# An attention and expert kernel on one core: the attention loop written out, four pieces of a step in another place

## The chip, the core and the metric

The kernel runs on one core of a Trainium2 chip. The time is the device time of one execution in microseconds, and the median of several executions is what counts. Before the change it is 2137.03 us, the median of three runs (2134.46 to 2138.43). TensorE (PE) multiplies, VectorE (DVE), ScalarE (ACT) and GpSimd (POOL) do the rest, and SyncE (SP) issues most of the transfers.

## The reference

Input `x` has 32 batches of 128 rows and 512 columns. The first half is attention with 32 heads of 16 columns, with a second set of keys and values from the adapter `ctx`; the second half is a mixture of 8 experts, of which each row uses two.

```python
q, k, v = (split_heads(layernorm(x) @ W) for W in (Wq, Wk, Wv))
q, k = rope(q), rope(k)
w = softmax(q @ k.T * D ** -0.5 + mask)
a_k, a_v = split_heads(ctx @ Wk), split_heads(ctx @ Wv)
a = tanh(gate) * softmax(q @ a_k.T * D ** -0.5)
x = x + merge_heads(w @ v + a @ a_v) @ Wo
h = layernorm(x)
top2, ids = top_k(h @ router_w.T, 2)
out = x + sum(softmax(top2)[j] * expert(ids[j], h) for j in (0, 1))
# expert(e, h) = (silu(gate_e(h)) * up_e(h)) @ w2[e].T
```

## The kernel before

`program` runs `attention_phase` and then `expert_phase`; the change is in the first alone. A batch is one tile of 128 rows. In float16 a product is made of three (high by high, high by low, low by high), so a projection of 512 columns is 12 matmuls (`project`, L1045), and a tensor that goes into one is first split: ACT writes the high half, POOL or DVE the difference.

Each engine has its own program. `walk` (L244) calls an engine's `step(b, c, d, n, m)` once for each batch b, with its neighbours: c is two batches back, d one back, n the next and m the one behind that. A step finishes batch b (softmax and values), projects the output of d and normalizes it (h), enters the rows of c in the lists of the experts, and prepares n (projections of queries, keys, adapter keys, stacks of heads, the maxima of the scores). Nothing but the order of the calls in `step` and the semaphores sets the order of the work: every engine takes its instructions in the order in which they stand. Steps 4 to 27 are a hardware loop of three rounds with eight steps each (`eng.Fori`, `LOOP`), all other steps are written out.

TensorE's step has 16 rounds u, one for each half group of heads: `scores_T` (L1143, L1147, L1152) writes scores in `st`, ACT takes their exponentials (`exps`, L561), and `values` for round u-1 (L1166) multiplies them by the values. Other pieces lie between: in round 2 `k` (projection of the keys of n, in `ma[1]`) ahead of values 1 and `out_turn` (the output's transposes, L1039, in `md[0]`) behind it; in round 3 `out_project`; in round 4 `ak` (adapter keys); `stack` (L1084) from round 6 on; `h_turn` in round 7 and `router` in round 8.

ACT's step is not touched by the diff. In round 2 it has, in this order, the third exponential (L561), `w_slice` (two passes over a slice of the experts' weights, L571 and L572) and `out_T` (L583), which copies the output's transposes to `oT` for `out_project`. Later come `k_high` (L539), `ak_high` (L519) in round 4, `h_high` (L589) in round 5, the first `values_T` (L567), the exponential of round 6, the first `stack_out` (L553, L555), the exponential of round 7, and `h_transposed` (L594), for which `router` waits. The exponential of round u waits for `scores_T` of round u.

VectorE's step has `router_top` (L838 to L861, the choice of two experts for c), `rotate_k` (L730, L734), `router_weights`, `residual` (L809 to L817), `router_counts` (L866, L868), `router_rows` (L906 to L915, places in the lists), `norm_h` (L824), `ak_low` (two L721, which `stack` 0 on TensorE waits for), `h_low` (L829), `norm_x` (L693), `normal` 0 (L786 to L798), `router_logits` (L833), and then the maxima (L754, L756, L759) of the eight groups. The adapter scores of group 0 (L1108) use the bank that `router_logits` reads, and wait for it.

GpSimd's step has `q_sum` (L410), `q_low` (L415), `w_slice` (L448), `k_sum` (L420), `norm_h`, `k_low` (L425), `x_low` (L405) and `enter_lists`.

Of the kernel before, what the change touches and what calls it, by code (L numbers as in the profile page):

```python
# [24 lines left out]
NB = 32  # L25
# [12 lines left out]
GROUPS = NH // 4  # L38
VW = HD + 1
VC = 32  # L40
LOOP = 8
LB = 4
SLOTS = 2 * T // P + NE - 1
TAB = 16
# [59 lines left out]
def attention_phase(nc, ctx, dram, keep):  # L104
# [139 lines left out]
    def whole(n):  # L244

        return isinstance(n.n, int) and n.n == 0

    def walk(eng, step, first, last):

        def near(b, lacks):
            step(b, *(None if d in lacks else b.shift(d) for d in (-2, -1, 1, 2)))

        first(Batch(0, 0))
        near(Batch(0, 0), (-2, -1))
        near(Batch(0, 1), (-2,))
        near(Batch(0, 2), ())  # L260
        near(Batch(0, 3), ())
        with eng.Fori(0, (NB - 8) // LOOP) as it:
            for k in range(LOOP):
                near(Batch(it, 4 + k, LOOP), ())
        near(Batch(0, NB - 4), ())
        near(Batch(0, NB - 3), ())
        near(Batch(0, NB - 2), (2,))
        near(Batch(0, NB - 1), (1, 2))
        last(Batch(0, NB - 1))

    def heads(t):
        return t[:, :].rearrange("p (h d) -> p h d", d=HD)
# [392 lines left out]
    def _(dve):  # L665
# [116 lines left out]
        def normal(n, o):  # L782

            bank = av[o % 2][:, :, :].rearrange("p (a g) (j c) -> p a (g j) c", a=2, c=VC)
            dve.wait_ge(v_back.sem, v_back.at(n, o + 1))
            dve.reciprocal(rc[:, :, :], bank[:, :, :, HD]).then_inc(n_rc.sem, 1)  # L786
            dve.wait_ge(n_rc.sem, n_rc.at(n, o + 1))
            dve.tensor_tensor(rc[:, 1, :], rc[:, 1, :], tg[:, 8 * o:8 * o + 8], ALU.mult).then_inc(n_rg.sem, 1)
            dve.wait_ge(n_rg.sem, n_rg.at(n, o + 1))
            dve.tensor_tensor(part2[:, :, :, :], bank[:, :, :, 0:HD],  # L790
                              rc[:, :, :].unsqueeze(3).to_broadcast([P, 2, 8, HD]), ALU.mult).then_inc(n_o2.sem, 1)
            dve.wait_ge(n_o2.sem, n_o2.at(n, o + 1))
            if o == 0:
                if whole(n):
                    dve.wait_ge(list_pad.sem(n), list_pad.at(n))
                dve.wait_ge(o_hi.sem, o_hi.at(n.shift(-1)))
                dve.wait_ge(o_lo.sem, o_lo.at(n.shift(-1)))
            dve.tensor_tensor(heads(on)[:, 8 * o:8 * o + 8, :], part2[:, 0, :, :], part2[:, 1, :, :],  # L798
                              ALU.add).then_inc(n_o.sem, 1)

        def out_low(n):
            dve.wait_ge(o_hi.sem, o_hi.at(n))
            dve.tensor_tensor(ohs[:, 1, :], on[:, :], ohs[:, 0, :], ALU.subtract).then_inc(o_lo.sem, 1)
# [15 lines left out]
        def norm_h(n, x_batch):  # L819
            dve.wait_ge(h_rs.sem, h_rs.at(n))  # L820
            if x_batch:
                dve.wait_ge(x_hi.sem, x_hi.at(x_batch))
                dve.wait_ge(x_lo.sem, x_lo.at(x_batch))
            dve.tensor_scalar(nat[:, :], x2[:, :], mv[:, 1, 0:1], mv[:, 1, 3:4], ALU.subtract,  # L824
                              ALU.mult).then_inc(h_n.sem, 1)

        def h_low(n):
            dve.wait_ge(h_hi.sem, h_hi.at(n))
            dve.tensor_tensor(ohs[:, 1, :], nat[:, :], ohs[:, 0, :], ALU.subtract).then_inc(h_lo.sem, 1)  # L829
# [64 lines left out]
        def router_rows(n):  # L894

            if whole(n):
                dve.tensor_scalar(unsel[:, :], sel[:, :], -1.0, 1.0, ALU.mult, ALU.add).then_inc(f_step.sem, 1)
                dve.wait_ge(f_step.sem, f_step.at(n, 1))
                dve.scalar_tensor_tensor(out=pos[:, :], in0=unsel[:, :], scalar=tok[:, 1:2], in1=pos[:, :],
                                         op0=ALU.mult, op1=ALU.add).then_inc(f_step.sem, 1)  # L900
                dve.wait_ge(f_step.sem, f_step.at(n, 2))
                dve.tensor_tensor(pos[:, :], pos[:, :], ebase[:, :], ALU.add).then_inc(f_step.sem, 1)
                dve.wait_ge(f_step.sem, f_step.at(n, 3))
                dve.tensor_copy(posi[:, :], pos[:, :]).then_inc(f_pos.sem, 1)
            else:
                dve.tensor_tensor(pos[:, :], pos[:, :], ebase[:, :], ALU.add).then_inc(f_step.sem, 1)  # L906
                dve.wait_ge(f_step.sem, f_step.at(n, 1))
                dve.tensor_tensor(chosen[:, :, :], oh[:, :, :], pos[:, :].unsqueeze(1).to_broadcast([P, 2, NE]),
                                  ALU.mult).then_inc(f_step.sem, 1)
                dve.wait_ge(f_step.sem, f_step.at(n, 2))  # L910
                dve.tensor_reduce(place[:, :], chosen[:, :, :], AX.X, ALU.add).then_inc(f_step.sem, 1)
                dve.wait_ge(f_step.sem, f_step.at(n, 3))
                dve.tensor_copy(posi[:, 0:2], place[:, :]).then_inc(f_pos.sem, 1)

            dve.tensor_scalar(tok[:, 0:1], tok[:, 0:1], float(P), None, ALU.add).then_inc(f_step.sem, 1)  # L915
            dve.wait_ge(f_step.sem, f_step.at(n, 4))

        def step(b, c, d, n, m):
            if n:
                ctx_lo(n)  # L920
                mask_lo(n)
                rotate_q(n)
            if d:
                out_low(d)
            if m:
                stats_x(m)
            if c:
                router_top(c)
            if n:
                rotate_k(n)  # L930
            if c:
                router_weights(c)
            if d:
                residual(d)
            if c:
                router_counts(c)
                router_rows(c)
            if d:
                norm_h(d, n)
            if n:  # L940
                ak_low(n)
            if d:
                h_low(d)
            if m:
                norm_x(m)
            normal(b, 0)
            if d:
                router_logits(d)
            if n:
                maxima(n, 0)  # L950
                maxima(n, 1)
            normal(b, 1)
            if n:
                for g in range(2, 6):
                    maxima(n, g)
            normal(b, 2)
            if n:
                for g in range(6, GROUPS):
                    maxima(n, g)
                neg_max(n, b)  # L960
            else:
                normal(b, 3)
# [72 lines left out]
    def _(pe):  # L1035
# [25 lines left out]
        def k(n):  # L1061
            pe.wait_ge(av_v.sem, av_v.at(n.shift(-1)))
            project(ma[1], xT, wk).then_inc(k_p.sem, 1)
# [113 lines left out]
        def out_turn(n):  # L1177
            pe.wait_ge(o_hi.sem, o_hi.at(n))
            pe.wait_ge(o_lo.sem, o_lo.at(n))
            transposes(md[0], ohs).then_inc(o_tp.sem, 1)  # L1180
# [24 lines left out]
        def step(b, c, d, n, m):  # L1205
            if n:
                q(n)
            for u in range(2 * GROUPS):
                scores_T(b, u)
                if u in BACK_AT:  # L1210
                    values_back(b, BACK_AT.index(u))
                if u == 2 and n:
                    k(n)
                if u == 3 and d:
                    out_project(d)
                if u == 4 and n:
                    ak(n)
                if u == 7 and d:
                    h_turn(d)
                if u == 8 and d:  # L1220
                    router(d)
                if n and u in STACK_AT:
                    stack(n, STACK_AT.index(u))
                if n and u in SCORES_AT:
                    adapter_scores(n, SCORES_AT.index(u))
                if u:
                    values(b, u - 1)
                if u == 2 and d:
                    out_turn(d)
                if u == 3 and c:  # L1230
                    places(c, n)
                if n and u in SCORES_AT:
                    own_scores(n, SCORES_AT.index(u))
            if n:
                v(n)
                adapter_scores(n, GROUPS - 1)
            values(b, 2 * GROUPS - 1)
            if n:
                own_scores(n, GROUPS - 1)
            if m:  # L1240
                x_turn(m)
            if n:
                avp(n)
            values_back(b, 3)
            if n:
                max_turn(n)
# [385 lines left out]
```

## Time and profile before

| | |
|---|---|
| median of three runs | 2137.03 us (2134.46 to 2138.43) |
| profiled execution | 2133.7 us, of which the span of the instructions is 2131.9 us |
| PE busy | 1900.5 us, 89% |
| DVE busy | 1452.3 us, 68% |
| ACT busy | 1219.3 us, 57% |
| POOL busy | 647.5 us, 30% |
| mean granted clock of TensorE | 0.975 |

The attention phase takes the first 1645 us or so and the experts the rest. In the written rows a time is a place on the span's clock. Busy shares are means over both phases; which engine ends a wait is read in the list of waits and in the timeline. Matmuls overlap, so the start of the next one lies a little ahead of the modelled end of the one in front.

### The profile page before, as it was taken

The page shows a single profiled execution, that of the slowest core. Times are in us where ns is not written, and L with a number is a line of the kernel's source. Part 1 is how long each engine was busy: PE and PEld are TensorE (multiplying, and loading weights), DVE is VectorE, ACT ScalarE, POOL GpSimd, SP SyncE. Part 2 cuts the span into 40 slices and gives each one's busy share as a digit, 9 for nine tenths or more (in the row PEclk, how much of TensorE's full clock was granted, in tenths as well). Part 3 has the DMA queues.
Part 4 walks back from the last instruction along what each step waited for, and adds up shares of the span by engine and source line. Part 5 has one row for each costly group of instructions (what it writes and reads, how often), then busy time and mean ns, then how long its engine had stood idle before and what let it go on. Part 6 is the DMA issues. An engine that isn't in the chain of part 4 may idle for free. (4 is left out here: it accounts for less than half of the span.)

```text
span 2131.9 us, 54083 instructions
## 1 busy us (share of the span) xinstructions
PE 1900.5 (89%) x18697; PEld 1172.2 (55%) x18698; DVE 1452.3 (68%) x3621; ACT 1219.3 (57%) x2228; POOL 647.5 (30%) x667
## 2 busy tenths in 40 slices
PE   4898899989998999999899999999983799999997
PEld 2555555555554555555555555555551466666664
DVE  5577788888887888888788888888874333333332
ACT  4565566666665666666566666666662434434342
POOL 3123233222322222232222222222321344444443
PEclk8999999999999999999999999999996899999999
DMA  3011111111111111111111111111012444444443
GB/s 124 24 34 34 34 34 34 40 41 55 35 34 35 34 34 34 34 34 39 30 40 52 45 34 34 34 34 34 29 33 72 106 81 86 82 83 85 81 87 59
DMA packets 64040, 106.14 MB, mean 50 GB/s; under 512 B 19089, under 2 KB 23185, under 8 KB 63313
## 3 DMA queue, kind: packets, MB, share of 16 engines
q0 software_dynamic: 18144, 37.31, 9.7%
q1 hardware_dynamic: 45680, 65.96, 9.6%
q8 instruction: 136, 2.23, 0.4%
q14 instruction: 80, 0.65, 0.1%
HBM read 67.51 MB, written 35.72 MB: 48 GB/s over the span
## 5 line engine op out<-in xcount | busy, mean ns | idle before, releaser
L561 ACT ACTIVATE pr<-st 128x512 f32<-128x512 f32 x512 | 299.9, 592 | 202.9 <-PE st L1152 193.0
L1499 PE MATMUL y<-w1s,hgT 128*128 x1704 | 279.8, 314 | 3.7 <-ACT hgT L1413 3.7
L410 POOL TENSOR_TENSOR t<-t 128x512 f32<-128x512 f32 x32 | 50.4, 1575 | 668.6 <-DVE t L734 668.6
L754 DVE TENSOR_REDUCE mx<-md 128x4 f32<-128x512 f32 x256 | 176.6, 690 | 86.6 <-PE md L1108 71.9
L1166 PE MATMUL av<-pr,vv 128*17 128x128 f32 x4096 | 212.4, 278 | 17.5 <-ACT pr L561 17.1
L1499 PEld LDWEIGHTS y<-w1s,hgT 128*128 128x128 f16 x1704 | 164.4, 98 | 95.4 <-issue 4.1
L553 ACT ACTIVATE qz<-ma 64x256 f16<-64x256 f16 x512 | 191.7, 374 | 19.2 <-PE ma L1084 16.2
L1152 PE MATMUL st<-mT,hsel 96*128 96x128 bf16 x2048 | 201.8, 221 | 0.0
L1143 PE MATMUL st<-qz,kk 128*128 128x256 f16 x1024 | 197.8, 275 | 1.4 <-DVE mT L780 1.4
L759 DVE TENSOR_REDUCE mx<-md 128x4 f32<-128x512 f32 x256 | 177.0, 691 | 8.7
L1147 PE MATMUL st<-identr,mskp 128*128 128x512 f32 x512 | 182.3, 437 | 0.0
L1152 PEld LDWEIGHTS st<-mT,hsel 96*128 96x128 bf16 x2048 | 137.5, 98 | 75.7 <-issue 69.8
L756 DVE TENSOR_TENSOR md<-md,msk 128x512 f32<-128x512 f32 x256 | 177.1, 692 | 0.0
L1413 ACT ACTIVATE hgT<-px 128x1024 f16<-128x1024 f16 x71 | 72.7, 1024 | 155.7 <-PE px L1489 155.7
L555 ACT ACTIVATE kk<-ma 128x512 f16<-128x512 f16 x256 | 152.9, 597 | 3.0
L1518 PE MATMUL y<-w2s,yT 128*128 (+1 forms) x639 | 150.3, 379 | 0.9 <-DVE yT L1477 0.9
L1117 PE MATMUL md<-kk,qz 128*128 128x128 f16 x1024 | 101.1, 221 | 51.3 <-DVE mx L759 50.9
L1476 DVE COPY yT<-py 128x256 f16<-128x256 f16 x142 | 40.4, 284 | 148.2 <-PE py L1508 148.2
L405 POOL TENSOR_TENSOR xcs<-nat,xcs 128x512 f16<-128x512 f32 x31 | 36.0, 1162 | 300.3 <-ACT xcs L493 300.3
L1166 PEld LDWEIGHTS av<-pr,vv 128*17 128x17 f32 x4096 | 68.2, 95 | 103.2 <-issue 54.1
L1117 PEld LDWEIGHTS md<-kk,qz 128*128 128x128 f16 x1024 | 60.3, 97 | 110.1 <-issue 110.1
L1392 POOL DMA_INDIRECT out<-yo,dst x71 | 113.2, 1594 | 16.9 <-issue 12.6
(210 smaller groups left out, 3999.6 us busy)
## 6 DMA issues: line engine op xcount, KB each, us to landing
wst<-in_w SPq DMA_DIRECT2D x32, 352.0 KB, 3.2
cin<-in_ctx SPq DMA_DIRECT2D x32, 256.0 KB, 3.8
xin<-in_x SPq DMA_DIRECT2D x32, 256.0 KB, 3.4
xres<-in_x SPq DMA_DIRECT2D x32, 256.0 KB, 3.6
out<-x SPq DMA_DIRECT2D x32, 256.0 KB, 2.1
h_pairs<-ohs SPq DMA_DIRECT2D x32, 256.0 KB, 2.1
msk<-in_mask SPq DMA_DIRECT2D x32, 64.0 KB, 3.4
lrow<-lists SPq DMA_DIRECT2D x71, 1.0 KB, 3.5
```

The costliest lines, as they stand in the source:

```text
L553: act.activation(qz[r, pairs, j, :], bank[r, 0:2], ACT.Copy)
L555: act.activation(kk[:, :, pairs, :], keys, ACT.Copy).then_inc(stk_o.sem, 1)
L561: act.activation(pr[:, path, :, :], st[path][:, :, :], ACT.Exp).then_inc(p_ex.sem, 1)
L754: dve.tensor_reduce(mx[:, 1, 4 * g:4 * g + 4], sm[1][:, :, :], AX.X, ALU.max).then_inc(s_ad.sem, 1)
L756: dve.tensor_tensor(sm[0][:, :, :], sm[0][:, :, :], msk[:, n.par, :].unsqueeze(1).to_broadcast([P, 4, P]), ALU.add).then_inc(s_mask.sem, 1)
L759: dve.tensor_reduce(mx[:, 0, 4 * g:4 * g + 4], sm[0][:, :, :], AX.X, ALU.max).then_inc(s_own.sem, 1)
L1117: i = pe.matmul(sm[0][:, j, :], qz[:, h // 2, h % 2, :], kst[:, h // 2, :], start=True, stop=True)
L1143: pe.matmul(bank[:, 2 * j:2 * j + 2, :], keys[:, p, :], qz[:, p, :, :], start=(j == 0), stop=False, skip_group_check=True)
L1147: pe.matmul(bank[:, :, :], mskp[:, n.par, part, :], identr[:, :].unsqueeze(1).to_broadcast([P, 4, P]), start=False, stop=False, skip_group ...
L1152: i = pe.matmul(bank[:, j, :], hsel[:, h:h + 1].to_broadcast([3 * NH, P]), mT[:, path, :], start=False, stop=(j == 3), skip_group_check=True)
L1166: i = pe.matmul(av[u // 4 % 2][VC * j:VC * j + VW, 2 * path + g % 2, :], vv[:, n.par, path, h, :], pr[:, path, j, :], start=True, stop=True)
L1499: i = pe.matmul(y1[s.par][j][:, 0:F], hgT[:, s.par, a, c, :], w, start=(n == 0), stop=(n == 11))
```

## The change

The hardware loop of the attention phase goes: all 32 steps are written out. In TensorE's step `k` moves from round 2 to round 1, ahead of values 0, and `out_turn` from behind values 1 to ahead of them. In VectorE's step `ak_low` moves ahead of `norm_h`, and `router_rows` from ahead of `norm_h` to behind `normal` 0, just ahead of `router_logits`. ACT, GpSimd and SyncE keep their order. After the diff the line numbers of the new kernel are 9 lower in these functions.

```diff
--- before.py
+++ after.py
@@ -38,7 +38,6 @@
 GROUPS = NH // 4
 VW = HD + 1
 VC = 32
-LOOP = 8
 LB = 4
 SLOTS = 2 * T // P + NE - 1
 TAB = 16
@@ -255,17 +254,9 @@
             step(b, *(None if d in lacks else b.shift(d) for d in (-2, -1, 1, 2)))
 
         first(Batch(0, 0))
-        near(Batch(0, 0), (-2, -1))
-        near(Batch(0, 1), (-2,))
-        near(Batch(0, 2), ())
-        near(Batch(0, 3), ())
-        with eng.Fori(0, (NB - 8) // LOOP) as it:
-            for k in range(LOOP):
-                near(Batch(it, 4 + k, LOOP), ())
-        near(Batch(0, NB - 4), ())
-        near(Batch(0, NB - 3), ())
-        near(Batch(0, NB - 2), (2,))
-        near(Batch(0, NB - 1), (1, 2))
+        for n in range(NB):
+            b = Batch(0, n)
+            near(b, [d for d in (-2, -1, 1, 2) if not 0 <= n + d < NB])
         last(Batch(0, NB - 1))
 
     def heads(t):
@@ -934,16 +925,16 @@
                 residual(d)
             if c:
                 router_counts(c)
-                router_rows(c)
+            if n:
+                ak_low(n)
             if d:
                 norm_h(d, n)
-            if n:
-                ak_low(n)
-            if d:
                 h_low(d)
             if m:
                 norm_x(m)
             normal(b, 0)
+            if c:
+                router_rows(c)
             if d:
                 router_logits(d)
             if n:
@@ -1209,8 +1200,10 @@
                 scores_T(b, u)
                 if u in BACK_AT:
                     values_back(b, BACK_AT.index(u))
-                if u == 2 and n:
+                if u == 1 and n:
                     k(n)
+                if u == 2 and d:
+                    out_turn(d)
                 if u == 3 and d:
                     out_project(d)
                 if u == 4 and n:
@@ -1225,8 +1218,6 @@
                     adapter_scores(n, SCORES_AT.index(u))
                 if u:
                     values(b, u - 1)
-                if u == 2 and d:
-                    out_turn(d)
                 if u == 3 and c:
                     places(c, n)
                 if n and u in SCORES_AT:
```

The place of the first two moves, on TensorE, in the step that begins with the fourth projection of queries. `ma<-w_q,xT` and `ma<-w_k,xT` are the projections of queries and keys, `st` the scores, `av<-pr,vv` the values, `md<-ident,ohs` the output's transposes and `md<-w_o,oT` the output's projection. Before:

```order
L1152 MATMUL st<-mT,hsel 128x128 x4
L1166 MATMUL av<-pr,vv 17x128 x4
L1143 MATMUL st<-qz,kk 128x256 x2
L1147 MATMUL st<-identr,mskp 128x512 x2
L1152 MATMUL st<-mT,hsel 128x128 x4
L1045 MATMUL ma<-w_k,xT 128x512 x12
L1166 MATMUL av<-pr,vv 17x128 x4
L1039 MATMUL md<-ident,ohs 128x128 x8
L1143 MATMUL st<-qz,kk 128x256 x2
L1152 MATMUL st<-mT,hsel 128x128 x4
L1045 MATMUL md<-w_o,oT 128x512 x12
```

The same place now:

```order
L1143 MATMUL st<-mT,hsel 128x128 x4
L1036 MATMUL ma<-w_k,xT 128x512 x12
L1157 MATMUL av<-pr,vv 17x128 x4
L1134 MATMUL st<-qz,kk 128x256 x2
L1138 MATMUL st<-identr,mskp 128x512 x2
L1143 MATMUL st<-mT,hsel 128x128 x4
L1030 MATMUL md<-ident,ohs 128x128 x8
L1157 MATMUL av<-pr,vv 17x128 x4
L1134 MATMUL st<-qz,kk 128x256 x2
L1143 MATMUL st<-mT,hsel 128x128 x4
L1036 MATMUL md<-w_o,oT 128x512 x12
```

The keys' projection now stands ahead of the values and scores of rounds 0 and 2, and the transposes ahead of the values; the pieces between two projections are the same ones.

The place of the other two moves, on VectorE, in the same step. `count` and `pos` are the lists' counts and places, `nat<-x,mv` is `norm_h`, `aks` is `ak_low`, `lg<-md` the router's logits. Before:

```order
L868 TENSOR_TENSOR count<-ma,count 128x8
L906 TENSOR_TENSOR pos<-pos,ebase 128x8
L908 TENSOR_TENSOR chosen<-oh,pos 128x16
L911 TENSOR_REDUCE place<-chosen 128x2
L913 CAST posi<-place 128x2
L915 TENSOR_SCALAR tok<-tok 128x1
L824 TENSOR_SCALAR nat<-x,mv 128x512
L721 SCALAR_TENSOR_TENSOR aks<-ma,aks 128x32x16 x2
L829 TENSOR_TENSOR ohs<-nat,ohs 128x512
```

The same place now, to the logits:

```order
L859 TENSOR_TENSOR count<-ma,count 128x8
L712 SCALAR_TENSOR_TENSOR aks<-ma,aks 128x32x16 x2
L815 TENSOR_SCALAR nat<-x,mv 128x512
L820 TENSOR_TENSOR ohs<-nat,ohs 128x512
L684 TENSOR_SCALAR nat<-xin,mv 128x512
L777 RECIPROCAL rc<-av 128x16
L779 TENSOR_TENSOR rc<-rc,tg 128x8
L781 TENSOR_TENSOR part<-av,rc 128x256
L789 TENSOR_TENSOR on<-part 128x128
L897 TENSOR_TENSOR pos<-pos,ebase 128x8
L899 TENSOR_TENSOR chosen<-oh,pos 128x16
L902 TENSOR_REDUCE place<-chosen 128x2
```

The five instructions of the list rows left the place between the counts and `norm_h`, and `ak_low` now comes before `norm_h`, not behind it.

## Rows read from the trace of the kernel before

**Rows 1.** TensorE's waits, 160 to 1600 us: for whom, total us, times, longest.
```profile
PE md L1117 <- DVE mx L759: 43.4, 115, 0.6
...
PE ma L1045 <- issue: 9.2, 4, 2.8
```

**Rows 2.** Timeline, TensorE at the first loop restart and at the exit: start, us, instruction.
```profile
649.41 0.28 PE L1127 MATMUL md<-ident_bf,mp 128*96 128x128 bf16 x2
...
659.10 0.38 PE L1143 MATMUL st<-qz,kk 128*128 128x256 f16 x2
...
1437.51 0.28 PE L1127 MATMUL md<-ident_bf,mp 128*96 128x128 bf16 x2
...
1440.21 0.38 PE L1143 MATMUL st<-qz,kk 128*128 128x256 f16 x2
```

**Rows 3.** Timeline, TensorE in one step of the loop (553 to 601 us).
```profile
557.38 0.41 PE L1166 MATMUL av<-pr,vv 128*17 128x128 f32 x8 [0.40 <-ACT pr L561]
...
558.41 0.40 PE L1152 MATMUL st<-mT,hsel 96*128 96x128 bf16 x4
558.65 2.76 PE L1045 MATMUL ma<-w_k,xT 128*128 128x512 f16 x12
561.33 0.41 PE L1166 MATMUL av<-pr,vv 128*17 128x128 f32 x8
...
563.41 2.76 PE L1045 MATMUL md<-w_o,oT 128*128 128x512 f16 x12 [0.67 <-ACT oT L583]
...
573.58 0.27 PE L1084 MATMUL ma<-ident,qs 128*128 128x128 f16 x2 [1.12 <-DVE aks L721]
...
577.40 0.45 PE L1045 MATMUL md<-rw,hT 128*128 128x8 f16 x12
```

**Rows 4.** Timeline, ScalarE in step 31, which has no keys to project.
```profile
1586.41 0.60 ACT L561 ACTIVATE pr<-st 128x512 f32<-128x512 f32 x1 [1.05 <-PE st L1152]
...
1588.27 1.02 ACT L583 ACTIVATE oT<-md 128x1024 f16<-128x1024 f16 x1
```

**Rows 5.** Timeline, TensorE in step 31.
```profile
1585.98 0.40 PE L1152 MATMUL st<-mT,hsel 96*128 96x128 bf16 x4
...
1589.34 1.04 PE L1045 MATMUL md<-w_o,oT 128*128 128x512 f16 x4 [1.62 <-ACT oT L583]
```

**Rows 6.** Timeline, ScalarE in the step of rows 3.
```profile
570.22 1.02 ACT L519 ACTIVATE aks<-ma 128x1024 f16<-128x1024 f32 x1 [1.66 <-PE ma L1045]
...
572.16 0.63 ACT L589 ACTIVATE ohs<-nat 128x512 f16<-128x512 f32 x1 [0.43 <-DVE nat L824]
...
574.12 0.77 ACT L553 ACTIVATE qz<-ma 64x256 f16<-64x256 f16 x2 [0.35 <-PE ma L1084]
...
575.90 1.02 ACT L594 ACTIVATE hT<-md 128x1024 f16<-128x1024 f16 x1
...
587.41 0.60 ACT L561 ACTIVATE pr<-st 128x512 f32<-128x512 f32 x1 [1.24 <-PE st L1152]
```

**Rows 7.** Timeline, VectorE in the same step.
```profile
562.11 1.44 DVE L851 SCALAR_TENSOR_TENSOR key<-oh,key 128x8 f32<-128x8 f32 x1
...
571.58 0.55 DVE L824 TENSOR_SCALAR nat<-x,mv 128x512 f32<-128x512 f32 x1
572.05 1.28 DVE L721 SCALAR_TENSOR_TENSOR aks<-ma,aks 128x512 f16<-128x512 f32 x2
573.24 0.68 DVE L829 TENSOR_TENSOR ohs<-nat,ohs 128x512 f16<-128x512 f32 x1
...
577.88 0.17 DVE L833 COPY lg<-md 128x8 f32<-128x8 f32 x1 [1.19 <-PE md L1045]
```

**Rows 8.** Timeline, GpSimd in the same step.
```profile
562.00 1.52 POOL L448 TENSOR_TENSOR w1s<-wst,w1s 128x704 f32 x1
```

**Rows 9.** VectorE on `key` and on `posi`, 250 to 1600 us: ns min/median/max, first and last start.
```profile
L851 DVE SCALAR_TENSOR_TENSOR key<-oh,key x28: 166/1441/2016, 271.9 to 1585.9; 128x8 f32<-128x8 f32 x28
...
L913 DVE CAST posi<-place x28: 168/1958/1978, 279.3 to 1594.8; 128x2 int32<-128x2 f32 x28
```

More of the change, by code:

```diff
@@ L936, in step @@
                 router_counts(c)
-                router_rows(c)
-            if d:
-                norm_h(d, n)
             if n:
@@ L942, in step @@
             if d:
+                norm_h(d, n)
                 h_low(d)
```

## The prediction

> **What bounds the kernel now.** I read the list of waits first, then the timeline of one ordinary step, then the loop's restarts. In the attention phase TensorE waits little: its largest total is for VectorE's maxima, 43.4 us in 115 waits of at most 0.6, and 9.2 us in four waits are for its own instructions [rows 1]. In one step I see three waits that the change aims at: 0.40 us at values 0 for the first exponential, 0.67 at the output projection for `oT`, 1.12 at the first stack for `aks` [rows 3], 2.19 in all. Everything else there is TensorE's own work, so a step ends later or sooner by what these waits become, as long as nothing behind them takes over. The maxima are a chain that starts when `router_logits` has read its bank, so a delay of the router moves the rest of the step. Nothing in the expert phase is touched.
>
> **The loop.** From the maxima's transposes (L1127) to the first scores (L1143) there is only the queries' projection. At the exit to the written steps this takes 1440.21 - 1437.51 = 2.70 us. At the first restart it takes 659.10 - 649.41 = 9.69, so 6.99 more [rows 2]. Three rounds have two restarts, and the four waits for instructions, 9.2 us, are two at each [rows 1]; I put the second at the same price, 14.0 together. At least the waits' 9.2 must go; a slow stretch behind a restart could make it 15. Code that is written out has no restart. Its cover is the fetch of instructions in a row; if that failed, the whole gain would go (a rival below).
>
> The Trainium skill (Runtime: NRT & Kernel Launch, Instruction fetch mechanics) says that a taken branch out of the window breaks the fetch, while crossing a block's boundary in sequence costs little that is not hidden. By it two branches are paid for here, as in my sum, and the exit shows no price, which agrees; it speaks against the rival that the written code streams worse.
>
> **Keys ahead of values 0.** The work up to the output projection is the same, in another order. Before, values 0 started at 557.38 after a wait of 0.40, so round 1's scores ended at 556.98; a projection starts 0.16 ahead of the modelled end in front of it (558.41 + 0.40 - 558.65), so the keys now start at 556.82. Values follow 2.68 later (561.33 - 558.65), at 559.50, with no wait: the 0.40 goes. From values 0 to the last piece of round 2's scores are 1.03 (558.41 - 557.38), and that piece ends 0.40 later, at 560.93 [rows 3]. What was ahead of the keys is now 2.1 us later, and ScalarE needs it.
>
> **Output transposes sooner.** In step 31 there are no keys, so ScalarE's order alone decides: the third exponential starts 0.03 after the scores end (1585.98 + 0.40 to 1586.41), the two passes of `w_slice` follow, `out_T` starts at 1588.27, and the projection at 1589.34, after TensorE waited 1.62 [rows 4, 5]. That is 2.93 from the exponential to the projection, and earlier transposes shorten none of it, because `out_T` stands behind the two passes. Now: 560.93 + 0.03 + 2.93 = 563.89, against 563.41 [rows 3]. The projection starts 0.48 **later**, although TensorE is ready sooner. From both sides: if the scores of round 2 were not what releases the exponential, the wait of 0.67 could go (-0.67); if the exponential starts another 0.15 later than in step 31 (an estimate), +0.63. I take +0.48, which is counted from one and the same chain in step 31.
>
> **Low adapter keys ahead of h.** Everything on TensorE from the projection to the adapter keys moves by 0.48. `ak_high` ended at 571.24 and now ends at 571.72 [rows 6]; VectorE has nothing before it, since the list rows have gone from there, and starts the two L721 at about 571.77 where it was 572.05. The stack follows 1.53 later (573.58 - 572.05), at 573.30 [rows 7, 3]: 0.28 sooner than before, with a wait of 0.36 left of 1.12. This is the whole gain of two moves, and it is not kept. `norm_h` now stands behind: it starts 1.19 after the first L721 (573.24 - 572.05) and takes 0.55 [rows 7], until 573.51; `h_high` starts at 573.54 instead of 572.16 [rows 6], 1.38 later. ScalarE has no room there: `h_high` to the first `stack_out` is 1.96 with 0.35 idle, thus 1.51 when its instructions overlap by their usual 0.1, and from there to `h_transposed` 1.78 [rows 6]. So `h_transposed` starts at 573.54 + 1.51 + 1.78 = 576.83 instead of 575.90. A projection follows such a copy by 1.07 (1588.27 to 1589.34) [rows 4, 5]: the router at 577.90 against 577.40 [rows 3], **0.50 late**. Either end alone gives what was lost at the output projection back to the step: I take +0.49 for a step. Bounds: -0.28 if the router did not wait, +0.93 if ScalarE's whole lag stayed.
>
> **List rows later.** Of the five instructions L913 is the dear one: 1958 ns at the median, 168 at least [rows 9]. Behind `normal` 0 GpSimd does no arithmetic, so all five should take an estimated 1.0 us (five of some 0.17 and their waits). VectorE had 1.19 us idle ahead of `lg` [rows 7], and `lg` is due 0.5 later now; its own work from `norm_h` on is later too, by up to 1.4, of which its idle time ahead of the values takes a part. I see about 0.5 of room left (an estimate), so the cost is nothing. If that cover is gone, each 0.1 over it is 3 us in all. On GpSimd `enter_lists` stands last and gains or loses nothing; the stores of h and the load of the weights' slice behind them on SyncE's queue start about 1 us later, and are wanted 20 us on.
>
> L851 takes 1.44 us, the time that GpSimd's L448 runs beside it (562.00 to 563.52) [rows 7, 8], and 166 ns at least [rows 9]. GpSimd's L448 waits for `w_slice` on ScalarE, which is 1.2 later now, so L851 should be through before it and VectorE gets to `rotate_k` 1.2 us sooner. That is worth nothing, as `residual` then waits for the later projection.
>
> The Trainium skill (SBUF — State Buffer, SBUF: two separate sides) calls the pair of ports that VectorE and GpSimd share a lock held for a whole instruction by whichever starts first. The rows of L851 and L448 look so. By it both held instructions shrink, and the time stays.
>
> **Sum.** 30 steps (1 to 30) have both d and n: 30 x 0.49 = 14.7 later. The loop gives 14.0. The span goes from 2131.9 to 2132.6, the profiled execution with the 1.8 us around it from 2133.7 to 2134.4, and since the median before is 3.3 above its profiled execution, the median to 2137.7, say **2138**. From no change one can tell about 0.2%, 4.3 us.
>
> **Rivals.**
> - *The loop's gain stays, faster.* The router's lateness is a difference of sums of ScalarE, and a few tenths decide it. If it isn't late, a step gains the stack's 0.28: 30 x 0.28 + 14.0 = 22 less, 2115. For it: the stack's wait is seen, and the router's was none. Against it: rows 6 show ScalarE without idle time there. If half of that holds, some 2126.
> - *All three waits go, much faster.* 30 x 2.19 + 14.0 = 80 less, 2057. Against it speaks the 2.93 of step 31.
> - *ScalarE's lag is carried on, slower.* Behind `h_transposed` ScalarE is 0.93 late and TensorE 0.50. ScalarE catches up in its idle time at the thirteenth exponential, 1.24 [rows 6]. If a `stack_out` or an exponential before that is waited for, a step costs the full 0.93: 28 - 14 = 14 more, 2151. It decides from the point where TensorE needs a stack less than 0.43 after ScalarE has it. For it: ScalarE works without a pause from the first stack on. Against: the banks let TensorE run a round ahead.
> - *The written code gives nothing back, slower.* If the fetch costs what the restarts did, only the 14.7 is left: 2152. The exit at 1437 us into written steps, 2.70 as anywhere [rows 2], speaks against it.
>
> **Chances.** Forecast 0.48 (within 0.2%: 0.33, faster 0.07, slower 0.08, as an error of 0.15 us in a step is 4.5 us); loop's gain stays 0.24; all waits go 0.02; lag carried on 0.20; code gives nothing 0.06. So faster 0.33, same 0.33, slower 0.34. The forecast's own range is 2128 to 2148; to hold 8 in 10 it must reach into the cases of both signs: 2116 to 2153.
>
> **What would show it.** In the profile after: no wait of 2 us or more for instructions at L1036, and the first scores 2.7 us behind L1118 in every step; the wait of values 0 gone; the output projection's wait for `oT` up from 0.67 to about 1.8, some 50 us in all; the stack's wait down to about 0.4; a new wait of about 0.5 at the router for `hT`; the cast to `posi` and L842 (L851 before) at 0.17 us; an ordinary step about 0.5 longer. The prediction is wrong if the projection's wait doesn't grow, if the router doesn't wait, or if VectorE's logits stand behind the list rows.

## The result and the profile after

The changed kernel takes 2140.27 us (median of 20 runs, 2135.92 to 2144.39), the kernel before 2134.51 us (20 runs, 2131.37 to 2139.16): a ratio of 1.0028 [1.0021, 1.0034], some 6.0 us (4.5 to 7.3) slower. The profiled execution has a span of 2137.6 us where it was 2131.9. Here and below two single executions that stand far off, one of the kernel before (5687 us) and one of the kernel with the transposes back (4733 us), are left out of the comparisons.

First the engines' line of the page after, and one group of its part 5:

```profile
PE 1907.9 (89%) x18697; PEld 1172.3 (55%) x18698; DVE 1344.0 (63%) x3621; ACT 1216.3 (57%) x2228; POOL 645.8 (30%) x667
...
L1036 PE MATMUL md<-w_o,oT 128*128 128x512 f16 x384 | 93.8, 397 | 51.0 <-ACT oT L574 51.0
```

VectorE is 108 us less busy (it was 1452.3), with the same 3621 instructions, and the kernel is slower: less busy time on VectorE did not by itself shorten the path. The list of TensorE's waits, 160 to 1610 us (for whom, total us, times, longest in us):

```profile
PE md L1036 <- ACT oT L574: 48.3, 30, 1.6
PE md L1108 <- DVE mx L750: 43.8, 116, 0.6
PE ma L1075 <- DVE aks L712: 10.7, 29, 0.4
PE md L1036 <- ACT hT L585: 9.7, 29, 0.3
...
PE av L1157 <- issue: 0.3, 1, 0.3
```

It answers to [rows 1]: the 9.2 us of waits for instructions are gone, and the largest wait is now that of the output projection for `oT`, 1.6 us thirty times. TensorE's timeline in the step that [rows 3] showed, here from 560.50, and below it the first scores behind the transposes of the maxima and one odd projection at 1402 us:

```profile
560.50 2.75 PE L1036 MATMUL ma<-w_q,xT 128*128 128x512 f16 x12
...
567.14 0.41 PE L1157 MATMUL av<-pr,vv 128*17 128x128 f32 x8
...
568.19 0.40 PE L1143 MATMUL st<-mT,hsel 96*128 96x128 bf16 x4
...
571.55 2.76 PE L1036 MATMUL md<-w_o,oT 128*128 128x512 f16 x12 [1.62 <-ACT oT L574]
...
580.97 0.27 PE L1075 MATMUL ma<-ident,qs 128*128 128x128 f16 x2 [0.37 <-DVE aks L712]
...
585.52 0.46 PE L1036 MATMUL md<-rw,hT 128*128 128x8 f16 x12 [0.33 <-ACT hT L585]
...
1390.72 0.27 PE L1118 MATMUL md<-ident_bf,mp 128*96 128x128 bf16 x2
...
1393.42 0.38 PE L1134 MATMUL st<-qz,kk 128*128 128x256 f16 x2
...
1401.89 4.45 PE L1036 MATMUL md<-w_o,oT 128*128 128x512 f16 x12 [1.62 <-ACT oT L574]
```

Read each start from the step's own (552.87 before, 560.50 after). Values 0 have no wait. The projection starts at 11.05 where it was 10.54, the first stack at 20.47 (20.71), the router at 25.02 (24.53). From L1118 to the first scores are 2.70 us. ScalarE in the same step:

```profile
568.63 0.60 ACT L552 ACTIVATE pr<-st 128x512 f32<-128x512 f32 x1 [1.17 <-PE st L1143]
569.12 0.78 ACT L562 ACTIVATE w1s<-wst 128x704 f16<-128x704 f32 x1
569.80 0.78 ACT L563 ACTIVATE wst<-wst 128x704 f32<-128x704 f32 x1
570.48 1.01 ACT L574 ACTIVATE oT<-md 128x1024 f16<-128x1024 f16 x1
...
581.20 0.63 ACT L580 ACTIVATE ohs<-nat 128x512 f16<-128x512 f32 x1 [1.32 <-DVE nat L815]
...
584.43 1.03 ACT L585 ACTIVATE hT<-md 128x1024 f16<-128x1024 f16 x1
```

ScalarE stands idle for 1.17 us ahead of the third exponential, so the delay of the output projection starts there: from the start of that exponential to the projection 2.92 us go by (571.55 - 568.63), with the two passes of `w_slice` (L562, L563) and `out_T` (L574) between. VectorE and GpSimd:

```profile
569.73 0.17 DVE L842 SCALAR_TENSOR_TENSOR key<-oh,key 128x8 f32<-128x8 f32 x1
...
579.43 1.29 DVE L712 SCALAR_TENSOR_TENSOR aks<-ma,aks 128x512 f16<-128x512 f32 x2 [2.98 <-ACT aks L510]
580.63 0.54 DVE L815 TENSOR_SCALAR nat<-x,mv 128x512 f32<-128x512 f32 x1
...
584.92 0.17 DVE L904 CAST posi<-place 128x2 int32<-128x2 f32 x1
...
586.08 0.17 DVE L824 COPY lg<-md 128x8 f32<-128x8 f32 x1 [0.94 <-PE md L1036]
```

```profile
570.66 1.52 POOL L439 TENSOR_TENSOR w1s<-wst,w1s 128x704 f16<-128x704 f32 x1 [0.99 <-ACT wst L563]
```

L842 (L851 before) ends before GpSimd's L439 begins, and takes 0.17 us where it took 1.44; the cast takes 0.17 for 1.96, and L883 (L892 before) 0.16 for 1.06. These three are most of the 108 us. From projection to projection of the queries a step is now 48.84 us, from 560.50 to 609.34, where it was 48.27 inside the loop.

**Where the 5.7 us of the two profiles stand.** Before, the two steps at each restart took 51.31 + 52.62 and 51.16 + 52.79, which is 14.8 over four ordinary ones. From the sixth projection of queries to the last (262.4 to 1534.2 before, 267.5 to 1539.1 after) both took 1272 us. Over these 26 steps the longer step costs 26 x 0.57 = 14.8, the odd projection at 1402 costs 1.7, the restarts give back 14.8, and seven other steps of before that were 0.2 to 0.3 longer than 48.27 give back 1.9: together 0.2 less. What is left is 5.1 in the first five steps and 0.8 behind the last. Of the first five, the second and the third are 1.3 longer each (44.14 for 42.82, 48.69 for 47.35), and so they are in the experiment with the loop put back (44.17 and 48.71): this 2.7 comes with the moves, and why it is more than 0.57 a step is not shown. The first, fourth and fifth differ by +1.7, -0.7 and +1.5. With the loop put back, where the same work stands in the same order, they differ from before by -0.2, 0.0 and -1.5, so this 2.5 is not shown to be the change's.

### The profile page after: what moved, and what is told of

It reads as the page before. It is cut to its first block and busy times, and to the rows that moved or that the text cites. A ratio compares the mean times of both kernels' runs of the same rounds, so it can differ in the third digit from the quotient of the medians.

```text
span 2137.6 us, 51748 instructions
## 1 busy us (share of the span) xinstructions
PE 1907.9 (89%) x18697; PEld 1172.3 (55%) x18698; DVE 1344.0 (63%) x3621; ACT 1216.3 (57%) x2228; POOL 645.8 (30%) x667
## 5 line engine op out<-in xcount | busy, mean ns | idle before, releaser
L1036 PE MATMUL md<-w_o,oT 128*128 128x512 f16 x384 | 93.8, 397 | 51.0 <-ACT oT L574 51.0
```

## The experiments

My theory was that of the prediction: the loop gives its restarts back, the keys ahead of values 0 delay a chain on ScalarE (third exponential, `w_slice`, `out_T`), and h behind the adapter keys makes the router late. The rivals were that the written code costs something of its own, that the list rows take room on VectorE, and that the transposes' place matters. Ratios are to the kernel before on the same chip, with the 95% interval in brackets. "Step" is the time from one projection of queries to the next in the steady part.

**The loop alone: before, written out.** Its edit and, for the four moves alone, the same edit undone in the changed kernel:

```diff
-        with eng.Fori(0, (NB - 8) // LOOP) as it:
-            for k in range(LOOP):
-                near(Batch(it, 4 + k, LOOP), ())
+        for n in range(NB):
+            b = Batch(0, n)
+            near(b, [d for d in (-2, -1, 1, 2) if not 0 <= n + d < NB])
```

> The kernel before with its attention loop written out, nothing moved. The main theory (restarts cost 7 us each and a little behind them; written steps stream freely; the moved pieces cost about 0.57 us a step): all ordinary steps at 48.3 us, no wait for instructions, about 14 to 15 us less than before, near 2120. Rival theory (written code costs as much as the restarts did, and the moves cost nothing): within 3 us of before, or slower.

> The changed kernel with the loop of before put back. Main theory: steps of 48.85 us and two restarts, 14 to 15 us more than the changed kernel, so 20 to 21 more than before, near 2155. Rival (the written code is what costs): near the kernel before, 2135 to 2140.

Written out: 2116.97 us, 0.9908 [0.9892, 0.9923], step 48.30. With the loop back: 2153.16 us, 1.0083 [1.0069, 1.0097], step 48.85, restarts 51.78 + 53.67 and 51.70 + 52.33. The waits of TensorE from 265 to 1490 us, of before written out:

```profile
PE md L1109 <- DVE mx L751: 37.8, 100, 0.6
PE ma L1076 <- DVE aks L713: 32.0, 25, 1.6
PE md L1037 <- ACT oT L575: 17.5, 26, 0.7
PE av L1158 <- ACT pr L553: 6.3, 26, 0.2
```

and of the changed kernel with the loop:

```profile
PE md L1044 <- ACT oT L582: 40.5, 25, 1.6
...
PE ma L1044 <- issue: 9.8, 4, 2.8
```

The waits for instructions come and go with the loop, and the 1.6 at `oT` stays with the moves. In neither written-out kernel does TensorE have a wait for instructions between 205 and 1610 us, so the rival that written code costs something of its own falls. With the loop the four moves cost 0.0083 x 2136 = 17.7 us. That this is near 30 x 0.57 = 17.1 is in part chance: of the 16.4 by which the two spans differ, 12.2 stand in the 26 steps (14.8 for the longer step, less 1.9 for the seven steps of before and 0.7 for the restarts), 1.1 in the first five and 3.1 behind the last. Writing out gives 0.0055 x 2136 = 11.7 us with the moves (1.0083 to 1.0028; 8 to 15 by the two intervals) and 19.6 without (16 to 23); the profiled spans give 10.7 (2148.3 to 2137.6) and 13.5 (2131.9 to 2118.4). The 13.5 is small because it compares single runs: that of before written out (2120.17) is the slowest of its four, 3.2 above their median, and that of before (2133.7) lies 2.4 below the median on that chip. Why the timed gain without the moves is the larger is open. Written out, values 0 wait 0.24 and not 0.40 in a step (in the kernel before, its written steps have the 0.24 and those of the loop the 0.40), but the stack then waits 1.26 and not 1.12: what comes sooner there is lost at `aks`.

**The keys back behind values 0.**

```diff
-                if u == 1 and n:
+                if u == 2 and n:
                     k(n)
```

> The changed kernel with the keys' projection back in round 2, ahead of the output transposes, which stay ahead of values 1. Main theory (keys ahead of values 0 delay the third exponential, and with it the slice's two passes and the copy of the output transposes): the projection's wait falls from 1.62 to about 0.3 us, the wait at values 0 is back at 0.4, the router waits 0.8 us for its copy, a step takes about 48.05 us; 2114 to 2118. Rival (the keys' place costs nothing, the wait saved at values 0 is kept): no gain, 2138 to 2145.

2101.45 us, 0.9835 [0.9821, 0.9848], step 47.75, less than the 48.05 that I expected, as values 0 and the router wait 0.24 and 0.35 and not 0.4 and 0.8. Its waits, 265 to 1490 us:

```profile
PE ma L1075 <- DVE aks L712: 9.5, 26, 0.4
PE md L1036 <- ACT hT L585: 9.1, 26, 0.3
PE av L1157 <- ACT pr L552: 6.0, 25, 0.2
PE md L1036 <- ACT oT L574: 5.8, 26, 0.2
```

The wait for `oT` falls from 1.62 to 0.22, below the 0.67 of before, since with the exponential back in its place `out_T` starts right behind `w_slice` and the sooner transposes do count here. The keys' place costs the changed kernel 1.10 us in each step (48.85 to 47.75).

**h ahead of the low adapter keys again; the slice's passes behind the copy; both.** The first is `norm_h` before `ak_low`. The second moves ScalarE's `w_slice` from round 2 to round 3, and GpSimd's part behind `k_sum`:

```diff
                 if u == 2:
-                    w_slice(b)
                     if d:
                         out_T(d)
                 if u == 3:
                     if c:
                         router_exp(c)
+                    w_slice(b)
```

> The changed kernel with the normalization of h back ahead of the low adapter keys; list rows stay late. Main theory (h behind the adapter keys makes ScalarE's chain to the router 1.4 us late): the router waits for nothing, the output projection still waits 1.6 us, a step takes about 48.1 us, 2115 to 2119. Rival (the low adapter keys' place is good, the stack's wait is what counts): the stack's wait of 0.37 grows again and the step is as long or longer, 2140 or more.

> The changed kernel with the two passes of the weights' slice on ScalarE moved from ahead of the copy of the output transposes to behind the router's exponential in round 3, and GpSimd's part of the slice from ahead of the keys' sum to behind it. Main theory (the copy stands behind the passes, that is the projection's wait): the projection waits about 0.45 us instead of 1.62, the router's wait for its copy grows to about 0.8, a step takes about 47.5 us, near 2100. Rival (the projection's wait is set by the exponentials or by TensorE's own transposes, not by the passes): the wait stays above 1.2 us and the time above 2130.

> The last kernel, and the normalization of h back ahead of the low adapter keys. Main theory (two separate delays, each needed): neither the projection nor the router waits more than 0.5 us, a step takes about 46.7 us, 2070 to 2078. Rival (one delay hides the other, or VectorE's maxima become the bound): no better than the better one of its two halves, 2095 or more.

h first: 2116.30 us, 0.9902 [0.9887, 0.9918], step 48.10. The slice later: 2090.76, 0.9790 [0.9776, 0.9803], step 47.50. Both: 2073.84, 0.9711 [0.9698, 0.9725], step 46.77. TensorE's waits with h first, 265 to 1490 us:

```profile
PE md L1037 <- ACT oT L574: 42.1, 26, 1.6
PE md L1109 <- DVE mx L750: 37.8, 100, 0.6
PE ma L1076 <- DVE aks L712: 9.2, 25, 0.4
```

The router's wait has gone and the stack's 0.37 has not grown: h behind the adapter keys bought nothing and costs 0.75 us a step. With both edits ScalarE, then TensorE:

```profile
548.43 0.60 ACT L552 ACTIVATE pr<-st 128x512 f32<-128x512 f32 x1 [1.17 <-PE st L1144]
548.92 1.02 ACT L574 ACTIVATE oT<-md 128x1024 f16<-128x1024 f16 x1
549.83 0.60 ACT L552 ACTIVATE pr<-st 128x512 f32<-128x512 f32 x1
550.40 0.80 ACT L562 ACTIVATE w1s<-wst 128x704 f16<-128x704 f32 x1
```

```profile
550.00 2.76 PE L1037 MATMUL md<-w_o,oT 128*128 128x512 f16 x12 [0.26 <-ACT oT L574]
...
559.42 0.27 PE L1076 MATMUL ma<-ident,qs 128*128 128x128 f16 x2 [0.37 <-DVE aks L712]
```

`out_T` stands right behind the exponential, 0.49 after its start and not 1.85, and the projection waits 0.26 and not 1.62: 1.36 of wait gone, 1.35 of step gone (48.85 to 47.50). In the steady step the two edits add up: 1.35 + 0.75 = 2.10, measured 2.08. In time they don't quite: 0.0238 + 0.0126 = 0.0364 by the two ratios, and 0.0317 measured for both, some 10 us less, which is more than the intervals allow. The three profiled spans do add up (48.3 + 15.6 = 63.9, measured 65.0), so the difference is not in these profiles and stays open.

**The same with the keys back in round 2.**

> The last kernel with the keys' projection back in round 2, behind the scores. Main theory (with the slice out of the way, keys ahead of values 0 are a gain, since they cover the first exponential and ScalarE is in time): 0.4 to 0.6 us a step longer than the last kernel, 12 to 18 us more. Rival (keys early are bad in themselves): shorter than the last kernel by 10 us or more.

2082.43 us, 0.9750 [0.9737, 0.9764], step 47.00, so 8.6 us slower than both edits alone. Once nothing stands between the exponential and `out_T`, keys ahead of values 0 are a gain of 0.23 a step (h stands first in both of these kernels; the pair with h behind was not run), less than the 0.4 to 0.6 that I expected: `oT` costs 0.22 with the keys late as well, and the only thing won is the 0.24 of values 0.

**The transposes back; the list rows back.**

```diff
-                if u == 2 and d:
-                    out_turn(d)
...
                 if u:
                     values(b, u - 1)
+                if u == 2 and d:
+                    out_turn(d)
```

> The changed kernel with the output transposes back behind values 1, nothing else. Main theory (their copy waits for ScalarE's passes, not for them): the same time as the changed kernel within 2 us, about 2140. Rival (earlier transposes feed the projection sooner): 0.35 us a step slower, some 10 us more.

> The changed kernel with the list rows back behind the counts, now ahead of the low adapter keys. Main theory (VectorE stands idle for 3 us there until ScalarE has the adapter keys, so even a held cast fits): a step of 48.85 us as in the changed kernel, the same time within 3 us, near 2140. Rival (the held cast delays the low adapter keys again): 0.7 us a step more, 2155 to 2162.

2140.58 us, 1.0023 [1.0014, 1.0033], step 48.83; and 2141.77 us, 1.0029 [1.0017, 1.0041], step 48.87. Neither differs from the changed kernel. The transposes are ready in either place before `out_T` may start. With the list rows back in front of `ak_low` the cast is at 1.96 us again, and yet VectorE waits for ScalarE's `ak_high`:

```profile
577.17 1.96 DVE L904 CAST posi<-place 128x2 int32<-128x2 f32 x1
...
579.70 1.29 DVE L712 SCALAR_TENSOR_TENSOR aks<-ma,aks 128x512 f16<-128x512 f32 x2 [0.52 <-ACT aks L510]
```

In the changed kernel the list rows have room in either place, because VectorE waits behind them in both, here 0.52 us for `ak_high` and there 0.94 for the router.

**VectorE's moves on before, written out.** First list rows later and `ak_low` ahead of `norm_h`, then the list rows alone, which is the edit shown:

```diff
             if c:
                 router_counts(c)
-                router_rows(c)
...
             normal(b, 0)
+            if c:
+                router_rows(c)
```

> The kernel before, written out, with both of VectorE's moves: low adapter keys ahead of h, list rows late. Main theory (what the stack gains is lost at the router, because h is late on ScalarE): a step of 48.3 to 48.45 us, within 4 us of the written-out kernel with nothing moved, near 2121, with a wait of about 0.7 us at the router. Rival (both moves gain): as good as with the list rows alone or better, 2098 or less.

> The kernel before, written out, with the list rows alone moved late (behind the first division of the values). Main theory: the cast to places takes 0.17 instead of 1.96 us, the low adapter keys start 0.7 us sooner while h is not late, so the stack and all behind it come 0.7 us sooner: a step of about 47.6 us, 20 to 24 us less than the written-out kernel with nothing moved, near 2098. Rival (VectorE's time there is off the path): the same time as that kernel, near 2120.

Both moves: 2116.89 us, 0.9912 [0.9898, 0.9925], step 48.20, which is the time of before written out. The stack's wait falls from 1.26 to 0.37 and the router gets one of 0.34. This kernel settles one thing more. It differs from the one with the keys back in the transposes' place alone: with the transposes behind values 1 the step is 48.20 and the wait for `oT` 0.67, ahead of them 47.75 and 0.22. So with the keys in round 2 the sooner transposes gain 0.45 us a step, and with the keys in round 1 nothing (48.83 and 48.84). The list rows alone: 2108.09 us, 0.9874 [0.9859, 0.9889], step 48.00: a gain of 0.30 a step, where I expected 0.7. VectorE in its step, then GpSimd:

```profile
565.39 2.35 DVE L816 TENSOR_SCALAR nat<-x,mv 128x512 f32<-128x512 f32 x1 [0.39 <-POOL mv L445]
567.67 1.27 DVE L713 SCALAR_TENSOR_TENSOR aks<-ma,aks 128x512 f16<-128x512 f32 x2
```

```profile
565.32 2.14 POOL L417 TENSOR_TENSOR ks<-t,ks 128x1024 f16<-128x1024 f32 x1
```

`norm_h` takes 2.35 us instead of the 0.54 it has above: it ends 0.28 behind GpSimd's `k_low`, where the cast before ended 0.03 behind it. Taking the held cast away hands the hold to `norm_h`, and the stack still waits 0.89. `ak_low` is not held in this way: with the keys back it started at 564.50, inside `k_low` (563.15 to 565.29), and its two instructions took the usual 1.29. In the changed kernel `ak_low` stands ahead of `norm_h` and waits for ScalarE until 579.43, when `k_low` (576.77 to 578.89) is over, so nothing is held.

**Another way to both: `out_T` ahead of the passes in round 2, GpSimd as it was, h first.**

> The changed kernel with two calls of ScalarE's round 2 exchanged (copy of the output transposes ahead of the slice's passes) and the normalization of h ahead of the low adapter keys; GpSimd keeps its order. Main theory (the copy's place behind the passes and h behind the adapter keys are the two delays): a step of 46.7 to 46.9 us, 2070 to 2078, as the kernel with the slice in round 3. Rival (the passes now delay the fourth exponential and GpSimd's keys' sum): 0.5 us a step more or worse, 2088 and up.

2083.17 us, 0.9756 [0.9742, 0.9770], step 47.03: 9 us slower than with the passes in round 3, where I expected the same time. The projection waits the same 0.26, though GpSimd's order is untouched here, so it is the place of ScalarE's passes that decides this wait. VectorE, GpSimd and the first stack on TensorE:

```profile
558.21 2.50 DVE L815 TENSOR_SCALAR nat<-x,mv 128x512 f32<-128x512 f32 x1 [0.39 <-POOL mv L444]
560.63 1.27 DVE L712 SCALAR_TENSOR_TENSOR aks<-ma,aks 128x512 f16<-128x512 f32 x2
```

```profile
558.30 2.13 POOL L416 TENSOR_TENSOR ks<-t,ks 128x1024 f16<-128x1024 f32 x1
```

```profile
562.16 0.27 PE L1076 MATMUL ma<-ident,qs 128*128 128x128 f16 x2 [0.65 <-DVE aks L712]
```

GpSimd gets to `k_low` at 15.5 into the step and with the passes in round 3 at 15.2 (555.50 - 540.30), and the instruction it holds ends that much later: the stack waits 0.65 and not 0.37, which is the difference of 0.26 between the two steps. The version with both edits (0.9711) stays the fastest of all.

## Why the prediction came out as it did

The time was inside the range, 2.3 us from the number, and part of that nearness is luck. The change forecast was +0.7 us and the measured one is +6.0. The number stood 2.5 us higher than that change would put it, because it started from a median of three runs (2137.03) and twenty runs have 2134.51. The forecast, no change to be told, missed by a little: the ratio stands at 1.0028 where its bound was 1.0020, on the slower side, to which the prediction gave 0.34. The mechanism came out piece by piece as follows.

- **The loop.** Right. No wait of 2 us for instructions is left, the scores come 2.70 behind L1118. The restarts gave 14.8 for the predicted 14.0. Seven steps of before that were 0.2 to 0.3 us longer than the others, which I had not looked for, gave another 1.9; they are gone without the loop, and gone too with the moves and the loop, so they are not shown to be the loop's. By the timed runs the loop cost 11.7 us with the moves (8 to 15) and 19.6 without (16 to 23).
- **Keys ahead of values 0.** Right, and the largest term: the wait of 0.40 went, and the projection came at +0.51 by its start for the predicted +0.48, with a wait of 1.62 for "about 1.8". Its total was 48.3 us for "some 50". Of the 0.40, the keys save only 0.24; the other 0.16 goes with the loop alone. That ScalarE's two passes are what it costs is shown by moving them away (1.36).
- **Sooner transposes.** Right: worth nothing in the changed kernel. What I did not see is that the keys' move is what makes it so: with the keys in round 2 they gain 0.45 a step.
- **Low adapter keys ahead of h.** Right step by step: the first stack at 20.47 into the step (predicted 20.43), `h_transposed` at 23.93 (23.96), the router at 25.02 (25.03), and its wait 0.33 for "about 0.5". What I undersold is that the late router is pure loss: undone, a step gains 0.75, more than the 0.50 by which the router is late, because the stack keeps its 0.37 either way once the list rows are gone from there. On before, where that room is missing, the same two moves cancel to nothing.
- **List rows later.** Right: 0.02 a step in the changed kernel.
- **The sum.** The step is +0.57 and not +0.49; this is the term that was mis-sized. The router is 0.49 late, as predicted, and the logits follow its start by 0.56 (586.08 - 585.52) where it was 0.48 (577.88 - 577.40), which is the missing 0.08; the first adapter scores, which wait for the logits' bank, then start 0.57 later (25.89 for 25.32 into the step). Over 30 steps it is 2.4 us. In the profiles the restarts and the seven longer steps gave 2.7 more than the 14.0, so these two cancel; the odd projection (+1.7) and the first and last steps (+3.6 beyond their share of the step's growth) make the 5.0 by which the two spans differ more than forecast. Of those 3.6, the second and third steps hold 1.5, which come with the moves; the other 2.1 are open.
- **Rivals.** "The loop's gain stays" needed a router that is on time; it waits 29 times. "All three waits go" needed a projection without a wait; it waits 1.62. "ScalarE's lag is carried on" needed +0.93; the step shows 0.57, so ScalarE's lag was not carried on in full. "The written code gives nothing back" is refuted by both experiments on the loop.

## What to carry to other kernels

Moving a matmul group earlier moves what was there later: ask which engine's in-order queue starts its next long chain from the displaced piece, and clear that chain (here two passes of 0.78 us that could as well stand behind it) before making the move; the same move was a loss of 1.10 us a step with the passes in the chain, and a gain of 0.23 with the passes out of it and h first. A good edit can be hidden by a bad one made with it: the sooner transposes gained 0.45 us a step alone and nothing beside the early keys, so time each edit alone and together. A hold is not always cured by moving the held instruction away: look which one takes its place beside the holder.

## What was not expected of the hardware

**A short wait and a slow stretch.** The projection at 1401.89 took 4.45 us and not 2.76. The stretches of the changed kernel around an ordinary step and there (length, busy time of PE, PEld, DVE, ACT, POOL, granted clock, DMA share, GB/s):

```profile
560.50:609.30 48.80, 44.78 (x483) 27.38 (x482) 36.70 (x94) 31.55 (x61) 12.94 (x11) 1.00 0.11 37
...
1400.00:1404.00 4.00, 2.38 (x11) 0.92 (x9) 2.67 (x12) 2.41 (x5) 3.01 (x4) 0.75 0.00 0
```

The granted clock is 1.00 in one and 0.75 in the other: for part of the second TensorE was at 1.2 and not at 2.4 GHz, and the step took 50.53 instead of 48.84. From 265 us to the end of step 30 in each profile, the loop's restarts left out, such stretches stand only behind a wait of 1.62 us: one in the changed kernel, five with h first, two with the transposes back and three with the list rows back, each behind the wait for `oT`; and one in before written out, behind a single wait of 1.62 for `aks`. In the seven experiments whose waits for `oT` and `aks` are all 1.3 or less there, and in the kernel before (at most 1.41), none did; nor did one in the changed kernel with the loop, which has the 1.62. So such a wait was at times followed by a loss of another 1.7 us, but mostly not, and what decides it was not settled.

**A hold in spite of the earlier start.** In the last experiment `norm_h` started at 558.21, before GpSimd's `k_low` at 558.30, and still ended with it, 2.50 us long. The Trainium skill (SBUF — State Buffer, SBUF: two separate sides) gives the shared pair of ports to whichever of the two starts first. By that rule `norm_h` should have taken its 0.54 us here; the measurement says otherwise, as far as two starts only 0.09 us apart can be told in a profile whose spans on GpSimd are rough.

**A standstill near 215 us.** In all fourteen profiles TensorE, VectorE and ScalarE stop once together in the fifth step: before, ScalarE and VectorE resume at 216.1 and 216.0 after 7.1 and 6.7 us idle, in the changed kernel at 221.3 and 221.2 after 8.6 and 8.2. It is there with the loop and without, and ScalarE's idle time in it is 5.6 to 8.6 us, differing from kernel to kernel. The profile names no engine of this core that ends it. Its cause was not looked for by an experiment and is open.
